# Layer 0's expert rows: added to two DRAM sums in place of three, in an eight-block model on one core

## What is computed

```python
x = x + tanh(g_xattn[0]) * L0_xattn(layernorm(x), ctx, ...)        # attention
x = x + tanh(g_ffn[0])   * L0_ffn(layernorm(x), ...)               # 64 experts, 8 per token
x = x + tanh(g_xattn[1]) * L1_xattn(ctx, layernorm(x), ...)        # state-space scan, gated by layernorm(x)
x = x + tanh(g_ffn[1])   * L1_ffn(layernorm(x), ...)
...                                                                # layers 2 and 3
```

```python
probs = softmax(x2 @ gate_w.T); top_w, top_i = top_k(probs, 8)
# each expert takes up to C = 128 of the tokens that chose it
h = silu(xg @ w_gate) * (xg @ w_up)              # per expert, 128 rows x 128
y = h @ w_down                                   # per expert, 128 rows x 256
out = zeros(T, d).at[tok].add(y[loc] * flat_w)   # every token gets its 8 weighted rows
```

## Time and profile before

| | us |
|---|---|
| median of 3 runs | 1290.53 (1279.2 to 1292.67) |
| the profiled execution | 1280.51 |
| its span, first to last instruction | 1278.8 |
| first gather of the experts | 98.36 |
| first and last scatter issued | 120.82 and 349.08 |
| POOL busy | 674.6 (53%) |
| PE busy | 1072.3 (84%) |

### The profile page before, as it was taken

How to read it: one execution, slowest core, us unless ns; L and a number is a source line. 1 busy time by engine, 2 the same in 40 slices (tenths; PEclk the granted TensorE clock), 3 DMA queues, 4 the chain that set the end, 5 groups by cost and what they waited for, 6 DMA issues and landing times.

```text
span 1278.8 us, 18231 instructions
## 1 busy us (share of the span) xinstructions
PE 1072.3 (84%) x5382; PEld 838.8 (66%) x5382; DVE 819.2 (64%) x1515; ACT 678.0 (53%) x1718; POOL 674.6 (53%) x452
## 2 busy tenths in 40 slices
PE   6576788877647988999999999799989746999993
PEld 3456677666414665888888888665546445888883
DVE  3882799789778751656566665859998583333332
ACT  4476545444554225777777878557754125333331
POOL 2106888888823122445444445419997013786653
PEclk8888799899967997999999999979989857999997
DMA  6494899887440013011101110305441994777655
GB/s 189 141 196 129 233 284 295 229 255 173 54 132 1 1 34 94 28 57 48 57 19 54 51 52 2 103 1 154 137 138 52 259 268 133 177 165 134 101 74 130
DMA packets 153171, 154.49 MB, mean 121 GB/s; under 512 B 35188, under 2 KB 140396, under 8 KB 153076
## 3 DMA queue, kind: packets, MB, share of 16 engines
q1 hardware_dynamic: 129092, 123.04, 33.3%
q0 software_dynamic: 22896, 29.24, 14.0%
q10 hardware_dynamic: 1088, 1.05, 0.2%
HBM read 123.11 MB, written 30.18 MB: 120 GB/s over the span
## 4 chain that ended last, share of the span: by engine, by line
PE 55%; POOL 15%; DVE 11%; DMA 8%; issue 7%; ACT 3%; SPq 0%; POOLq 0%; DVEq 0%; ACTq 0%
PE bank L2495 8%; POOL f_sums L1023 6%; DMA f_sums<-arena,put 5%; PE bank L1599 4%; PE bank L1695 4%; PE bank L1662 4%; PE bank L1684 4%; POOL arena L1009 3%; PE bank L2124 3%; PE bank L1588 2%; PE bank L1617 2%; PE bank L1673 2%; PE bank L2515 2%; PE bank L2513 2%; POOL arena L560 2%
## 5 line engine op out<-in xcount | busy, mean ns | idle before, releaser
L540 DVE TENSOR_TENSOR_SCAN arena<-arena 128x1024 f32<-128x1024 f32 x64 | 154.4, 2412 | 20.4 <-issue 12.6
L1023 POOL DMA_INDIRECT f_sums<-arena,put x64 | 126.4, 1975 | 24.5 <-issue 16.2
L560 POOL TENSOR_TENSOR arena<-arena 128x1024 f32<-128x1024 f32 x32 | 82.5, 2579 | 94.5 <-DVE arena L540 94.5
L2392 POOL DMA_INDIRECT e_sums<-ctxT,put x63 | 98.7, 1567 | 55.0 <-DVE ctxT L2694 33.5
L1009 POOL DMA_INDIRECT arena<-y_rows,slots x64 | 83.0, 1297 | 65.1 <-DVEq L1224 45.9
L518 ACT ACTIVATE arena<-arena,ssm_A 128x255 f32<-128x255 f32 x256 | 108.0, 498 | 0.2
L2124 PE MATMUL bank<-yT,arena 128*128 128x512 f32 (+1 forms) x224 | 105.6, 617 | 2.2 <-ACT arena L2055 2.2
L2495 PE MATMUL bank<-arena,ssm_y 128*128 x504 | 107.1, 356 | 0.3 <-issue 0.3
L2688 DVE TENSOR_TENSOR ssm_y<-ssm_y,bank 128x256 f32<-128x256 f32 x63 | 26.5, 421 | 112.7 <-ACT ssm_y L2570 112.7
L570 PE MATMUL bank<-arena,ident 128*128 128x256 f32 x256 | 69.8, 420 | 34.1 <-DVE arena L560 32.1
L529 DVE TENSOR_TENSOR arena<-arena 128x1024 f32<-128x1024 f32 x64 | 93.7, 1464 | 0.0
(11 more groups left out here) (343 smaller groups left out, 2729.4 us busy)
## 6 DMA issues: line engine op xcount, KB each, us to landing
arena<-bc_rows SPq DMA_DIRECT2D x64, 512.0 KB, 5.2
y<-e_sorted SPq DMA_DIRECT2D x62, 128.0 KB, 2.5
arena<-in_L_ffn_w_gate_dram SPq DMA_DIRECT2D x16, 256.0 KB, 3.8
arena<-in_L_ffn_w_up_dram SPq DMA_DIRECT2D x16, 256.0 KB, 4.4
arena<-in_L_ffn_w_down_dram SPq DMA_DIRECT2D x16, 256.0 KB, 5.4
x<-in_L_ffn_w_gate_dram SPq DMA_DIRECT2D x16, 256.0 KB, 3.9
y<-in_L_ffn_w_up_dram SPq DMA_DIRECT2D x16, 256.0 KB, 4.6
yT<-in_L_ffn_w_down_dram SPq DMA_DIRECT2D x16, 256.0 KB, 5.5
```

The lines of the kernel that those rows point to most:

```text
L540: nc.vector.tensor_tensor_scan(ssm_h[:, j % 2, :], ssm_decay[:, j % 2, :], ssm_in, 0.0, ALU.mult, ALU.add).then_inc(s_ssm_h, 1)
L560: ops.tensor_tensor(ssm_hC_buf[:, j % 2, :], ssm_h[:, j % 2, :], ssm_C[:, g % 2, :], ALU.mult).then_inc(s_ssm_hC, 1)
L1023: nc.gpsimd.indirect_dma_start(out=f0_sums[m % SUMS], out_offset=bass.IndirectOffsetOnAxis(ap=put[:, m:m + 1], axis=0), in_=f0_ye[:, n % R ...
L2392: nc.gpsimd.indirect_dma_start(out=e_sums[t % 2], out_offset=bass.IndirectOffsetOnAxis(ap=put[:, t:t + 1], axis=0), in_=e_ye[:, t % 4, :], ...
```

## The change

`SUMS` goes from 3 to 2. Scatter m now goes to sum m % 2, and follows the landing of scatter m - 2. One sum less is cleared (one write of the 1024 token rows and one of the spare rows), so `CLEARS` goes from 8 to 6. SP brings back sum 0 alone, ACT's queue sum 1, and DVE has one add for each batch in place of two. POOL's order of gathers and scatters stays as it was.

```diff
-        SUMS = 3
+        SUMS = 2
...
-        CLEARS = 8
+        CLEARS = 6
...
             for b in range(B):
                 tiles = slice(TPB * b, TPB * (b + 1))
-                for a, rows in enumerate(f0_sums[0:2]):
-                    dst = x if a == 0 else f0_more[:, a - 1, :].rearrange("p (i d) -> p i d", d=D)
-                    sp.dma_start(dst[:, tiles, :], rows[0:T, :].rearrange("(i p) d -> p i d", p=P)[:, tiles, :]
-                                 ).then_inc(s_f0_more[b], 16)
+                sp.dma_start(x[:, tiles, :], f0_sums[0][0:T, :].rearrange("(i p) d -> p i d", p=P)[:, tiles, :]
+                             ).then_inc(s_f0_more[b], 16)
...
                 dve.wait_ge(s_f0_more[b], 16 * SUMS)
                 rows = x[:, TPB * b:TPB * (b + 1), :].rearrange("p a n -> p (a n)")
                 more = f0_more[:, :, TPB * b * D:TPB * (b + 1) * D]
-                dve_link(nc.vector.tensor_tensor(rows, rows, more[:, 0, :], ALU.add))
-                nc.vector.tensor_tensor(rows, rows, more[:, 1, :], ALU.add).then_inc(s_f0_x, 1)
+                nc.vector.tensor_tensor(rows, rows, more[:, 0, :], ALU.add).then_inc(s_f0_x, 1)
```

## The result

The changed kernel takes 1294.62 us (median of 20 runs, 1287.57 to 1302.93), the kernel before 1285.39 us (20 runs, 1274.68 to 1292.67). The ratio is 1.0091, with a 95% interval from 1.0073 to 1.0108. That is 11.7 us (9.4 to 13.9) of 1285.39; the two medians as they stand lie 9.2 us apart, and the text goes by the ratio. The change made the kernel a little slower, just inside the 1% that the prediction took as the bound. Its profiled execution spans 1289.4 us, 10.6 more than the one shown of before.

What follows compares the result with a forecast made beforehand. POOL's unbroken gathers and scatters were taken to bound the expert stage. Waits paid of +7.2 us, -2.4 on the way back and 0 for clears gave +4.8; on the median 1290.5 that made 1295 us, range 1282 to 1311.

Steps and rivals of the forecast that it cites:

- The base: Whole kernel: the median of the runs shown, 1290.5 us, to which the forecast change of +4.8 us was added.
- The prediction's own marks: Changed profile: 7 to 12 us of POOL waits, last scatter 5 to 9 us later; wrong if waits exceed 15 or under 3.
- The waits on POOL: Expert stage: fifteen scatters wait for scatter m - 2's landing, 11.6 us together, 9.8 of it in the part with gathers.
- with 0.15 us for that: POOL in the expert stage: a truly waiting scatter starts 0.15 us behind the landing it waits for.
- What the scans absorb: POOL in the expert stage: 38% of the waits pass during DVE scans, leaving 7.2 of 11.6 us paid.
- The way back: Behind the last scatter: fewer transfers and adds take 2.4 us off the path to DVE's L633, bounds 0 and 4.0.
- whose last copy ends at 369.43 whether there are two sums or three: ACT's line L402, L448, L454 behind the last scatter: its end stays at 369.43, so L618 gains at most 1.4 us.
- The clears: SP's start of the kernel: one 1 MB write and one small one less end inside existing cover, 0 us.
- Rival A: Stretch from 130 to 310 us: landings grow, waits feed each other, +17 to +26 us, 1308 to 1317; chance 0.24.
- Rival B: Expert stage: two sums suffice, landings 1 us shorter, -0.5 to -2 us, 1289; chance 0.15.
- Rival C: Scatters are held by something else; only start and end gain, -2.4 us and the clears, 1288; chance 0.06.

Runs made afterwards that it cites:

- wait2: Kernel before, three sums all cleared and brought back, but POOL waits for scatter m - 2 in place of m - 3: 1294.14 us, ratio 1.0088.
- sp2: Changed kernel, but SP's queue brings back both sums, so ACT neither waits for the last landing nor issues: 1288.86 us, ratio to the kernel before 1.0055.
- read2: Kernel before, but only sums 0 and 1 brought back and added, sum 2 left out of the result: ratio 0.9982.
- sp3: Kernel before, but SP's queue brings back all three sums in place of sharing them with ACT's queue: ratio 0.9983.
- early: Kernel before, but scatters 60 to 63 go to sums 0 and 1; ACT's queue brings back sum 2 early, SP the others: ratio 1.0009.
- after: The changed kernel itself, two sums, in its first profile, against the kernel before: 1294.62 us, ratio 1.0091.
- after_again: The changed kernel run once more, unaltered, for a second profile, against the kernel before: ratio 1.0090.
- wait1: Kernel before, three sums, but POOL waits for scatter m - 1 to land before every scatter: one run, 1398.79 us.
- noscan2: Changed kernel, two sums, with DVE's 32 expert-stage scans left out: 1275.74 us, ratio to the kernel before 0.9962.
- noload2: Changed kernel, two sums, with the weights of pairs 8 to 31 not loaded: ratio to the kernel before 1.0034.

## Why the prediction was right, and where its sizes were off

The direction, the range and the mechanism came out. POOL bounds the stage, scatter m - 2's landing is what scatter m now waits for, and wait2 shows that this alone gives the whole loss. That the 1295 lies so near the measured 1294.62 is luck: two errors cancel. The base, the median of three runs, was 1290.5, and over 20 runs it is 1285.4, 5.1 us less. (The profiled execution, 1280.51, lies 1.3 us above the lowest of the three; the prediction calls them equal.) And the forecast of +4.8 us is less than half of the measured 11.7 (9.4 to 13.9).

The prediction's own marks say the same. The true waits of the changed kernel are 15.5 and 27.4 us in its two profiles, over the 15 us that it set as the sign of a wrong forecast; the last scatter starts 13.9 us later (363.0 to 349.08) in place of 5 to 9; L618 does start right behind L454, but L633 isn't 2.4 us nearer to the last scatter, only 0.5. The landings are as it said in wait2 (6.4 us among the gathers) and a little under it in sp2 (5.9). Three terms of its sum have now been measured. The means are over the four profiles each with three sums and no added wait (before, read2, sp3, early) and with the wait for m - 2 (after, after_again, sp2, wait2).

**The waits on POOL**, forecast 11.6 us: measured 19.2 in the mean (13.6 to 27.4; 1.2 of it for ACT's results), against 0.4 with three sums. The step that failed is "with 0.15 us for that", the time from a landing to the start behind it. It was taken from one wait, scatter 19's, read as 193.72 less a landing rounded to 193.5 (0.2 us, and 0.15 in the sum), and scatter 19 is the second of its pair. wait1 shows 0.27 us for a second scatter and 0.73 at the least for a first one, which most of those that wait are. The same replay of the timeline of before with 0.73 and 0.27 us gives 20 waits and 19.5 us in place of 15 and 11.6, 14.7 of them up to scatter 51, so the landings could be kept as they were: that part of the method held. For three sums the same replay adds 0.05 us to the one short wait that their timeline has. That 19.5 meets the mean of four profiles so closely is partly luck too, since they spread by 14 us.

**What the scans absorb**, forecast 38%: measured 26%. POOL's rows sum to 198.3 us with three sums and to 193.4 with the wait, 5.0 us less, beside 18.8 us more of waits. The 26% is loose: rows of three sums alone spread over 7 us, and between the one profile of before and the first of the change the difference is 0.7. noscan2 shows it from the other side, since without scans nothing is absorbed. The net of the two terms was forecast as 7.2 us; the stage is 233.2 us with three sums and 247.0 with the wait, 13.8 us more.

**The way back**, forecast -2.4 us: measured -2.7 in read2, but -0.5 and +0.1 in the two profiles of the change itself. The step that fell is "whose last copy ends at 369.43 whether there are two sums or three": ACT's line stands behind PE's L433 and L440, and with a granted clock of 0.63 in place of 0.81 these take 11.7 us in place of 8.9, so L454 ends later than the normed rows by so much that the gain is used up. I had no such term. Both profiles of the change, wait2, sp2, sp3 and early had 0.63 from the start of L433 to the end of L454; the other eight had 0.81 to 0.84. The two kernels that bring back two sums with a clock over 0.8, read2 and noload2, have L633 at 20.8 and 20.6 us, so the gain is there when the clock is. Why the clock is lower wasn't found; it doesn't follow the number of sums (sp3 has three). PE sat idle ahead of L433 for 4.0 to 8.5 us in five of the six with 0.63, and for 9.2 us or more in the eight others (10.4 in before, 27.2 in wait1), but after_again, with 11.8 us of idle time and 0.63, doesn't fit. These are one or two profiles of each kernel, and the other executions have no such rows.

**The clears** were counted at nothing. No run tested them alone; SP still had its last clear out long before its next wait, and wait2, with all of them, is as slow as the change.

**Rival A** (the waits feed each other through ACT and the weight loads, 1308 to 1317 us) didn't happen in that size, though its 19.5 to 28.6 us of waits were the right size for the first of its terms. It named longer landings as the cause, and these didn't come: 6.4 us among the gathers in wait2, as before, and 5.9 in sp2. What made the waits longer than 11.6 us was the start behind the landing, and a part was absorbed. **Rival B** fails by wait2: the wait for m - 2 costs the whole 11 us, and its landings weren't 1 us shorter. **Rival C** fails by POOL's waits.

The sum with the measured terms is 18.8 - 5.0 and about 0 for the way back, 13.8 us; the measured time is 11.7. In the one pair of profiles L633 is 13.4 us later (372.62 to 386.04) and the span 10.6. The 2.8 us between weren't followed, and lie within what two executions of the same kernel differ by.

## What to carry to other kernels

Before a wait is made stricter, replay the bounding engine's timeline with it: start, duration and landing of each transfer are there, and the sum of the waits came near the mean of the profiles once the start behind a landing was right. Take that start-up from several true waits of the same form, and keep apart instructions that stand behind different numbers of semaphores, because a wait that is always met shows nothing of it. And when transfers on the way back get fewer, follow the other lines that start from the same landing: the one that was second becomes the bound (here ACT's; taken off the landing, it let the gate start 4.8 us sooner).

## What was not expected of the hardware

A POOL DMA behind a truly awaited landing starts after 0.27 us where its own sum's semaphore is all that it waits for, and after 0.73 us or more where another wait stands before that (wait1). An indirect DMA of POOL whose row begins during a DVE scan is held until about the scan's end: of 34 such rows in the kernel before 32 end behind it, a gather by 0.8 us and a scatter by 1.4, while the other two began within 0.05 us of the scan. A row that began before the scan isn't held by it. DVE's products of the same size hold rows in the same way, for less time. Leaving out the 32 scans made POOL's rows 28 us shorter (198.3 to 169.9) and the whole kernel 25.2 us faster. TensorE's granted clock in the same stretch of the program was 0.81 to 0.84 in eight profiles and 0.63 in six, which moved work of 8.9 us to 11.7.
